# Splitting each expert pair's weights where they are used, and starting the routed stage one shared chunk earlier

## The reference

```python
x = x + 0.5 * ffn(layernorm(x)); x = x + attn(layernorm(x)); x = x + 0.5 * ffn(layernorm(x))

# ffn(flat), flat [4096, 128]
probs = softmax(flat @ gate_W.T)
top_v, top_i = top_k(probs, 2)
out_e  = (silu(flat @ w1_e[e]) * (flat @ w3_e[e])) @ w2_e[e]
routed = sum(gates[:, e] * out_e[e])
shared = sum((silu(flat @ w1_s[n]) * (flat @ w3_s[n])) @ w2_s[n]) / 8
return 0.5 * shared + 0.5 * routed

# attn(x)
q, k, v = split(rms_norm(x) @ w_qkv.T); q = rms_norm(q); k = rms_norm(k)
y = sigmoid(q) * cumsum(exp(k) * v) / (cumsum(exp(k)) + 1e-6)
u, g = split(y @ w_swiglu.T); return x + (u * silu(g)) @ w_out.T
```

## Time and profile before

| | us |
|---|---|
| median of 3 runs | 748.2 (746.82 to 748.32) |
| the profiled execution, its time | 750.38 |
| the profiled execution, its span | 748.7 |
| PE busy | 664.1 (89% of the span) |
| DVE busy | 463.5 (62%) |
| POOL busy | 445.3 (59%) |
| ACT busy | 411.0 (55%) |
| mean granted clock of PE | 0.963 of full speed |

### The profile page before, as it was taken

The page is one execution under the profiler, slowest core; times in us unless marked ns, Lnnn a source line. Parts: engine busy times, 40 slices in busy tenths (PEclk is TensorE's granted clock), DMA queues, the critical chain, the costliest instruction groups (busy, mean ns, idle before and its releaser), DMA issues.

```text
span 748.7 us, 14295 instructions
## 1 busy us (share of the span) xinstructions
PE 664.1 (89%) x4860; PEld 604.9 (81%) x4860; DVE 463.5 (62%) x1169; ACT 411.0 (55%) x861; POOL 445.3 (59%) x519
## 2 busy tenths in 40 slices
PE   3878929999999999966887777999999999999996
PEld 3667829999999999944664565788999999999973
DVE  6678884555444555447999885975455545454435
ACT  2658504666666666326664526663666666666520
POOL 5600396677777777459997515006577777777530
PEclk9989959999999999989999997999999999999998
DMA  9551001112222132031100000602121221112146
GB/s 299 217 88 27 2 15 44 43 50 55 53 53 54 51 55 54 30 123 42 42 30 1 0 1 1 116 2 44 36 55 55 51 54 51 54 53 52 39 130 228
DMA packets 35686, 45.91 MB, mean 61 GB/s; under 512 B 6433, under 2 KB 27937, under 8 KB 35233
## 3 DMA queue, kind: packets, MB, share of 16 engines
q1 hardware_dynamic: 25632, 24.39, 11.5%
q0 software_dynamic: 9984, 20.63, 11.3%
HBM read 28.41 MB, written 16.58 MB: 60 GB/s over the span
## 4 chain that ended last, share of the span: by engine, by line
PE 66%; DVE 20%; ACT 3%; issue 3%; POOL 3%; DMA 2%; SPq 1%; POOLq 0%; DVEq 0%; ACTq 0%
PE psY L1487 18%; PE psU L1336 6%; PE psU L1335 6%; PE psU L1334 6%; PE psG L1334 6%; PE psG L1336 6%; PE psG L1335 6%; PE psH L1405 5%; DVE rec L1076 3%; PE psT L1433 2%; DVE XN L747 2%; DVE hs L757 2%; DVE ln_stats L734 1%; DVE xn L1060 1%; POOL results L650 1%
## 5 line engine op out<-in xcount | busy, mean ns | idle before, releaser
L1155 ACT ACTIVATE silu<-psG 128x512 f32<-128x512 f32 x220 | 131.1, 596 | 168.3 <-PE psG L1336 147.9
L635 POOL DMA_INDIRECT rows<-tokens,source x156 | 150.3, 964 | 104.4 <-issue 45.3
L954 DVE TENSOR_TENSOR hT<-silu,psU 128x512 f32<-128x512 f32 x156 | 107.4, 688 | 157.9 <-PE psU L1336 151.5
L650 POOL DMA_INDIRECT results<-yout,target x156 | 153.4, 983 | 64.0 <-issue 45.7
L1487 PE MATMUL psY<-W,hT 128*128 x1232 | 162.3, 275 | 1.8 <-DVE yout L980 1.8
L1487 PEld LDWEIGHTS psY<-W,hT 128*128 128x128 f32 x1232 | 150.4, 191 | 2.1 <-DVE hT L954 2.1
L1229 ACT ACTIVATE w_high<-W13H 128x1024 fp32r x78 | 82.7, 1060 | 55.5 <-PE psU L1336 55.4
L1334 PE MATMUL psG<-xTH,w_high 128*128 128x256 f32 x312 | 100.0, 321 | 0.0
L1336 PE MATMUL psG<-xTH,w_low 128*128 128x256 f32 x312 | 88.0, 282 | 0.0
L1336 PE MATMUL psU<-xTH,w_low 128*128 128x256 f32 x312 | 88.0, 282 | 0.0
L1335 PE MATMUL psU<-xTL,w_high 128*128 128x256 f32 x312 | 87.7, 281 | 0.0
(11 more groups left out here) (188 smaller groups left out, 1245.3 us busy)
## 6 DMA issues: line engine op xcount, KB each, us to landing
W<-w_e SPq DMA_DIRECT2D x3, 2048.0 KB, 13.8
tokens<-XN SPq DMA_DIRECT2D x16, 260.0 KB, 6.0
Y<-results SPq DMA_DIRECT2D x32, 128.0 KB, 2.2
YF<-results SPq DMA_DIRECT2D x16, 256.0 KB, 5.7
rows<-tokens,source POOLq DMA_INDIRECT x156
results<-yout,target POOLq DMA_INDIRECT x156, 2.3
X<-x SPq DMA_DIRECT2D x8, 256.0 KB, 5.5
out<-X SPq DMA_DIRECT2D x8, 256.0 KB, 2.8
```

The lines of the kernel that those rows point to most:

```text
L635: pool.indirect_dma_start(rows[:, slot(l, g), t, :], None, tokens, bass.IndirectOffsetOnAxis(ap=source[:, tile:tile + 1], axis=0))\
L650: pool.indirect_dma_start(results, bass.IndirectOffsetOnAxis(ap=target[:, tile:tile + 1], axis=0), yout[:, g % 2, t, :], None).then_inc(y_ ...
L954: dve.tensor_tensor(hT[:, s.u // PT % 2, half, :].rearrange("p f c -> p (f c)"), silu[:, s.u % 2, :], psU[:, s.u % 2, :], ALU.mult).then_i ...
L1155: act.activation(silu[:, s.u % 2, :], psG[:, s.u % 2, :], ACT.Silu).then_inc(silu_done, 1)
```

## The change

`FRONT` becomes `[6, 5]`: one chunk of shared steps moves from ahead of the routed stage to behind it, in each layer. The copies `W13H` and `W13L` and the instructions that make them go. `W13` stays in fp32, with a memory of its own, and each pair's weights are split on the way to their homes: ACT rounds 128x1024 of `W13` into `w_high`, and DVE subtracts that from `W13` into `w_low`. For this DVE, too, loads each pair's offset into a register. The rounding of the transposed rows (`xTH`) goes from DVE to ACT. The first two pairs are split before the routed stage begins: on ACT after shared step 22 in layer 0 and 18 in layer 1, on DVE after the front's last step. `w_high`, `w_low` and the buffer `Y` share the memory of `YF`. POOL no longer has anything between the low parts of the tokens and its fetches.

```diff
-WCOLS = 1024
-WPARTS = E * F // WCOLS
-FRONT = [7, 6]
+FRONT = [6, 5]
...
-        W13H = sb("W13H", [P, 2, E * F], fp32r)
-        memory = overlaid([("W13", [P, 2, E * F], fp32)], [("YF", [P, TOPK, TILES, D], fp32)],
-                          [("W13L", [P, 2, E * F], fp32r)])
+        W13 = sb("W13", [P, 2, E * F])
+        memory = overlaid([(f"w_{part}{n}", [P, 2, F], fp32r) for n in range(2) for part in ("high", "low")] +
+                          [("Y", [P, 4, TOPK, TB, D], fp32)], [("YF", [P, TOPK, TILES, D], fp32)])
...
-                if l == 0:
-                    pool.wait_ge(place_made, BATCHES_P)
-                    for j in range(2 * WPARTS):
-                        w, cols = j % 2, bass.ds(j // 2 * WCOLS, WCOLS)
-                        pool.wait_ge(high_made, j + 1)
-                        pool.tensor_tensor(W13L[:, w, cols], W13[:, w, cols],
-                                           W13H[:, w, cols].bitcast(fp32), ALU.subtract).then_inc(w_split, 1)
...
-                    dve.tensor_copy(xTH[:, par, :, :].rearrange(flat), psT[:, :]).then_inc(xT_link, 1)
-                    dve.wait_ge(xT_link, g + (GROUPS * l + 1))
+                    dve.wait_ge(xT_high, g + (GROUPS * l + 1))
...
+                def low_weights(p):
+                    if p >= PAIRS:
+                        return
+                    dve.wait_ge(pair_high, PAIRS * l + p + 1)
+                    dve.tensor_tensor(w_low[p % 2][:, :, :], W13[:, :, bass.ds(entries[p], F)],
+                                      w_high[p % 2][:, :, :].bitcast(fp32), ALU.subtract).then_inc(pair_split, 1)
...
+                    if k == front[l]:
+                        dve.wait_ge(w_off_done, l + 1)
+                        for p in range(PT):
+                            look_up(p)
+                            low_weights(p)
...
-                pipelined(dve, [(gated_routed, 4), (copy_y, 6), (copy_xT_later, 0)], RUN, 2 * GT,
+                pipelined(dve, [(look_up_later, 4), (gated_routed, 4), (copy_y, 6), (low_later, 4), (copy_xT_later, 0)], RUN, 2 * GT,
...
+                def high_xT(g):
+                    act.wait_ge(xT_psum, GROUPS * l + g + 1)
+                    act.activation(xTH[:, g % 2, :, :].rearrange("p t c -> p (t c)"), psT[:, :], ACT.Copy)\
+                       .then_inc(xT_high, 1)
+                def high_weights(p):
+                    if p >= PAIRS:
+                        return
+                    if p >= PT:
+                        act.wait_ge(u_full, first_routed[l] + PT * (p - 1))
+                    act.activation(w_high[p % 2][:, :, :], W13[:, :, bass.ds(entries[p], F)], ACT.Copy)\
+                       .then_inc(pair_high, 1)
...
-                    if l == 0 and part < 2 * WPARTS:
-                        cols = bass.ds(part // 2 * WCOLS, WCOLS)
-                        act.activation(W13H[:, part % 2, cols], W13[:, part % 2, cols], ACT.Copy).then_inc(high_made, 1)
+                    if k == front[l] + 1:
+                        high_xT(0)
+                    if k == min(TABLE_STEP[l] + 3, front[l] - 1):
+                        act.wait_ge(w_off_done, l + 1)
+                        act.wait_ge(experts_in, 48)
+                        for p in range(PT):
+                            look_up(p)
+                            high_weights(p)
...
                 for k in range(RUN):
+                    if k % PT == PT - 1:
+                        look_up(k // PT + PT)
                     silu_of(Step.of(k, 2), first_routed[l] + k)
-                    if k % PT == 1:
-                        weights_of(k // PT + PT, 0)
-                    elif k > 0:
-                        weights_of(k // PT - 1 + PT, 1)
+                    if k % GT == 0 and k // GT + 1 < GROUPS:
+                        high_xT(k // GT + 1)
+                    if k % PT == PT - 1:
+                        high_weights(k // PT + PT)
...
-                        pe.wait_ge(pair_weights, PT * (PAIRS * l + s.i // PT + 1))
+                        pe.wait_ge(pair_split, PAIRS * l + s.i // PT + 1)
```

More of the change, by code:

```diff
@@ L192, in macaron @@
         X = sb("X", [P, TILES, D])
-        W13H = sb("W13H", [P, 2, E * F], fp32r)
-        memory = overlaid([("W13", [P, 2, E * F], fp32)], [("YF", [P, TOPK, TILES, D], fp32)],
-                          [("W13L", [P, 2, E * F], fp32r)])
-        W13, W13L, YF = memory["W13"], memory["W13L"], memory["YF"]
+        W13 = sb("W13", [P, 2, E * F])
+        memory = overlaid([(f"w_{part}{n}", [P, 2, F], fp32r) for n in range(2) for part in ("high", "low")] +
+                          [("Y", [P, 4, TOPK, TB, D], fp32)], [("YF", [P, TOPK, TILES, D], fp32)])
+        w_high = [memory[f"w_high{n}"] for n in range(2)]
+        w_low = [memory[f"w_low{n}"] for n in range(2)]
+        YF, Y = memory["YF"], memory["Y"]
         W2 = sb("W2", [P, E * FT * D])
@@ L318, in macaron @@
              ("ha", [P, 2, TB * P], fp32)],
-            [("rows", [P, RING, GT, ROW], fp32),
-             ("gap", [P, 4 * CH * P - RING * GT * ROW], fp32),
-             ("w_low1", [P, 2, F], fp32r),
-             ("last_chunks", [P, (CHUNKS - 6) * CH * P], fp32),
-             ("w_high0", [P, 2, F], fp32r),
-             ("w_low0", [P, 2, F], fp32r),
-             ("w_high1", [P, 2, F], fp32r)],
+            [("rows", [P, RING, GT, ROW], fp32)],
             [("XNTL", [P, NT], fp32r), ("XNTH", [P, NT], fp32r)])
@@ L342, in macaron @@
         rows = memory["rows"]
-        w_high = [memory[f"w_high{n}"] for n in range(2)]
-        w_low = [memory[f"w_low{n}"] for n in range(2)]
         psG = ps("psG", [P, 2, 512])
@@ L955, in gated_routed, with look_up_later, low_later @@
                                       psU[:, s.u % 2, :], ALU.mult).then_inc(h_done, 1)
+                def look_up_later(s):
+                    if s.i % PT == PT - 1:
+                        look_up(s.i // PT + PT)
+                def low_later(s):
+                    if s.i % PT == PT - 1:
+                        low_weights(s.i // PT + PT)
                 def copy_xT_later(s):
@@ L1029, in _ @@
                     gated_shared(Step.of(k, 2 * FT))
+                    if k % FT == 6 % FT and k // FT > FRONT[0]:
+                        add_shared(k // FT - 1)
                 add_shared(CHUNKS - 1)
@@ L1216, in _ @@
                         batches += 1
-                def weights_of(p, part):
-                    if p >= PAIRS:
-                        return
-                    if part == 0 and p < PT:
-                        act.wait_ge(u_full, shared_at(l, (4 + 2 * p) * FT - 1) + 1)
-                    elif part == 0:
-                        act.wait_ge(u_full, first_routed[l] + PT * (p - 1))
-                    if p not in entries:
-                        entries[p] = act.value_load(w_off[0:1, p:p + 1], min_val=0, max_val=(E - 1) * F)
-                    kept, used = ((W13H, w_high), (W13L, w_low))[part]
-                    act.activation(used[p % 2][:, :, :], kept[:, :, bass.ds(entries[p], F)], ACT.Copy)\
-                       .then_inc(pair_weights, 1)
-                entries = {}
-                act.wait_ge(w_off_done, l + 1)
-                act.wait_ge(w_split, 2 * WPARTS)
-                for p in range(PT):
-                    weights_of(p, 0)
-                    weights_of(p, 1)
                 for k in range(RUN):
+                    if k % PT == PT - 1:
+                        look_up(k // PT + PT)
                     silu_of(Step.of(k, 2), first_routed[l] + k)
-                    if k % PT == 1:
-                        weights_of(k // PT + PT, 0)
-                    elif k > 0:
-                        weights_of(k // PT - 1 + PT, 1)
+                    if k % GT == 0 and k // GT + 1 < GROUPS:
+                        high_xT(k // GT + 1)
+                    if k % PT == PT - 1:
+                        high_weights(k // PT + PT)
                 for k in range(front[l], SHARED):
```

24 lines of the change are left out of this document (14 added, 10 removed).

## The result

| | before | after |
|---|---|---|
| median of 11 runs each, side by side | 748.25 us (746.82 to 749.54) | 750.3 us (748.12 to 750.9) |
| ratio | 1 | 1.0024, 95% interval 1.0012 to 1.0035 |
| profiled execution: time, span | 750.38, 748.7 | 750.3, 748.6 |
| mean granted clock | 0.963 | 0.979 |

The changed kernel is 0.24% slower, by about 2 us; 735.2 was predicted. The profiled execution of before lay 2 us above its median and that of after on its median, so a comparison of the two traces adds up to 0 and not to 2 us.

The account below looks back on a forecast made before the run. PE, busy 89% of the span, was taken as the bound, so gains come from its waits or clock. Terms −17.1 + 3.6 + 3.4 + 0.8 − 3.7 = −13.0 us took the median 748.2 to 735.2 us, range 730 to 744.

Parts of the forecast that it names:

- table of layer 0, its slow clock, ACT's batches: Layer 0's front: PE's 13.1 us wait, 2.8 of slow clock and 1.2 behind ACT's copies go; −17.1 us.
- wait for rows at the front's end: Before each routed stage: PE waits about 2.2 us for fetched rows; net +1.8 a layer, +3.6 us.
- slow clock after these waits: After the waits for rows: PE's clock at its lower level for 4 us, 1.7 a layer; +3.4 us, or 0.
- split in the routed stage: Routed stage: ACT's rounding and DVE's 1.2 us subtraction per pair leave PE's path unchanged; 0 us.
- POOL's pace: Routed stage: POOL takes 10.27 us a group against PE's 9.67 and has less lead; +0.4 a layer, +0.8 us.
- behind layer 0's routed stage: After layer 0's routed stage: the moved chunk's cover buys nothing, as attention already begins after the last shared chunk.
- tail of layer 1: End of layer 1: a third chunk covers the YF wait; 2.01 us wait and 1.7 slow clock go, −3.7 us.
- rival B: Routed stages: DVE's two-SBUF-input subtractions hold up POOL's DMAs; 34 us in all, 769 us; chance 0.12.
- 28d: Routed stage: each subtraction holds a POOL DMA for d, 2d a group over 14 groups; d taken as 0.6 us.
- a lead that is lived on: Routed stage: POOL falls back 0.6 us a group and lives on its start, in layer 1 13.5 us, then 6.5.
- 0.6 us to spare: Tightest place, the scaling at 284.13: results landed at 283.5; PE would bear some 0.5 us more.
- the first two pairs are covered: Front's end: splitting the first pairs takes 3.1 us beside PE's out_shared of 3.84; nothing, up to +1 a layer.

Follow-up runs that it names:

- e7: Kernel before, with the eight W13L subtractions made by DVE behind steps 20 to 27 of layer 0 instead of by POOL; 735.08 us.
- e1: Kernel after, but from the third pair on ACT also copies weights to psH in PSUM, and DVE subtracts w_high from that; 733.91 us, ratio 0.9814.
- e2: Kernel after, with w_low a plain DVE copy of W13 (one SBUF operand) instead of the subtraction; 747.02 us, ratio 0.9991.
- e6: Kernel of e1 (low parts from PSUM) with FRONT [7, 5] instead of [6, 5]; 732.57 us, ratio 0.9793.
- e4: Kernel after, with each DVE subtraction of 128x1024 made as two of 128x512; 749.41 us, ratio 1.0028.
- e3: Kernel after, with FRONT back at [7, 6] and each pair still split on its way by ACT and DVE; 746.59 us, ratio 0.9983.
- e8: Kernel of e3 with a ring of four groups of rows instead of three, results six groups behind; 747.82 us, ratio 0.9989.
- e9: Kernel of e8 with SEND_LAG = RING + 1, so results are again five groups behind the fetches; 746.2 us, ratio 0.9977.
- e11: Kernel after, with yout in three parts instead of two, a scaling waiting for the results of three groups before; 744.28 us, ratio 0.9948.
- e5: Kernel before, with w_low filled by DVE instead of ACT, by an operation of 128x1024 reading two SBUF operands; 776.29 us, ratio 1.0373.
- e10: Kernel of e6 with the rounding xTH given back to DVE, as in the kernel before; 732.46 us, ratio 0.9801.

## Why the prediction was wrong

By its own terms, measured in the two traces:

| term | predicted | measured |
|---|---|---|
| table of layer 0, its slow clock, ACT's batches | −17.1 | −17.1 |
| wait for rows at the front's end, net of 0.41, both layers | +3.6 | +3.3 |
| slow clock after these waits | +3.4 | 0 |
| split in the routed stage, and POOL's pace | 0 and +0.8 | +18.5 |
| behind layer 0's routed stage | 0 | −0.9 |
| tail of layer 1 | −3.7 | −3.9 |
| sum | −13.0 | −0.1 |

(−17.1 is 121.30 − 97.27 = 24.03, less the chunk of 9.08, plus the wait of 2.14. 18.5 is the 8.93 and 8.71 of the two routed stages plus the 0.41 a layer that had stood in them and belongs to the second row. The first row is not luck: it had been said as 13.1 + 2.8 + 1.2, and e7, which takes away the first two alone, measured 15.8. The −0.9 was not followed up; in that stretch the clock stood at its lower level from 328 to 335 us before, and from 324.5 to 328 after.)

**The step that failed** is the split in the routed stage, for which the sum takes 0. It looked at the path from ACT over DVE to PE, which indeed has room (PE never waits for `w_low`), and left POOL out of the sum. The price stood in rival B, and B's arithmetic holds: it had 28d a layer over the groups up to the tightest. With the measured mean d of 0.28 us (20.0 us over 72 holds) that is 7.8 us a layer, and the routed stages grew by 8.9 and 8.7. B said that it decides from d = 0.23. Its d of 0.6 was too large: since a held DMA ends 0.85 us behind the subtraction and takes 0.975 by itself, even random meetings would cost about 0.5 us each (an estimate from these rows), and they are not random, because the holds themselves set their phase. That 735.2 + 56 x 0.28 = 750.9 lies so near the measured 750.3 is partly luck: the slow clocks of +3.4 in it did not come, and the stages grew by more than 28d. So the forecast and B differed in one number that no row of before showed, and I gave B 12% because `gate_parts` had not lengthened a fetch. That was weak evidence, as the text itself said: an operation of 0.17 us is too short to show a hold, since even in one of 1.22 us a DMA that began 1.04 us into it took under 0.1 us more.

One reading that pointed the right way was at hand: DVE's table slowed to the length of POOL's subtractions, which shows that the two engines exclude each other. The fetch of 1.19 us beside the table says less than B made of it: the first fetch of layer 0 takes 1.17 us in the kernel after too (at 90.70), beside DVE's short operations at the end of the table. The Trainium skill (SBUF — State Buffer, Who interferes with whom) has both sentences that the prediction weighed. The one by which a DVE instruction with two SBUF inputs contends with GpSimd's reads holds here: 72 DMAs held by up to a microsecond. The one by which `tensor_tensor` did not stall DMAs does not, and the measurement decides. By the same section a DVE instruction with at most one input in SBUF, outside its fast modes, does not contend, and one in them does: e1 and e2 agree, with no hold and with holds of up to 0.4 us, if the copy of 128x1024 in 0.69 us is such a mode (the subtraction of 128x512 takes as long, 0.69 us in e4).

**POOL's pace** was right where nothing was held and the front was short: e1 shows one group of 10.1 us in each layer and e6 one in layer 1, the predicted 0.4. Its picture of a lead that is lived on was incomplete. The lead counts only up to the first send; after it POOL has the room of `yout`'s two halves (e3, e8, e9, e11). Hence the small step between "0.6 us to spare" and 9 us lost a layer: the room is used up once, and then each group shows in full.

**The slow clock** after the waits for rows was counted with 1.7 us each and did not come in the kernel after. Where it did come, in layer 1 of e11, it cost 1.6 us, so the size was right and its coming was not. The windows over both waits and what follows (us, PE busy, PEld, DVE, ACT, POOL, granted clock, DMA share, GB/s):

```profile
94.00:98.00 4.00, 1.86 (x12) 1.31 (x12) 2.30 (x4) 2.52 (x4) 3.09 (x4) 1.00 0.24 52
98.00:102.00 4.00, 4.00 (x38) 4.00 (x37) 3.19 (x6) 0.56 (x1) 3.08 (x4) 1.00 0.23 50
...
504.00:508.00 4.00, 2.04 (x14) 1.49 (x13) 2.79 (x4) 2.49 (x4) 3.04 (x4) 1.00 0.23 50
508.00:512.00 4.00, 4.00 (x38) 4.00 (x37) 2.95 (x6) 0.42 (x1) 2.84 (x3) 1.00 0.23 50
```

**All other steps held**: the first two pairs are covered, no wait of PE for `w_low`, `w_low` 1.22 us for an estimated 1.2, the wait for `YF` gone and the stretch from 710 to 740 at clock 1.00. Without the slow clock the sum is −16.4, which makes 731.8 us; e1, which has everything but the holds and groups 0.07 us longer (+2.5 us over 36 of them), took 733.9.

## What to carry to other kernels

Before work goes to DVE beside a POOL that issues indirect DMAs, look where its operands lie. An operation that reads SBUF alone can hold a DMA that starts inside it past its own end; the same operation with one operand in PSUM was free here, and a copy on ACT to get it there was cheap. And two engines that hold each other fall into step, so that the loss is not the mean of chance meetings: price it with both ends, and look for the buffer that gives the slower one its room (here `yout`), since a lead beyond it is worth nothing.

## What was not expected of the hardware

A hold ends at a fixed distance: in four kernels (after, e2, e3, e5) a held DMA's record ends 0.80 to 0.88 us after DVE's instruction, whatever its length (0.69 or 1.22 us) and wherever in it the DMA began, but for the first and last 0.05 us. In e5 those that began in the last tenth of a microsecond, which are hardly held at all, end up to 0.93 us after it.

PE's clock after a short wait is not told by the wait's length. In the kernel after, waits of 2.14 and 1.96 us left it at 1.00. In e11 a wait of 1.87 us at the same place in layer 1 was followed by slower work, `out_shared` in 5.04 us instead of 3.74, and in e10 one of 2.82 by this:

```profile
497.99 1.11 PE L1456 MATMUL psT<-ident,rows 128*128 128x128 f32 x4 [2.82 <-DMA rows<-tokens,source]
498.89 6.17 PE L1428 MATMUL psH<-W2S,hs 128*128 128x128 f32 x32
```

```profile
498.00:502.00 4.00, 4.00 (x19) 4.00 (x20) 3.02 (x6) 0.00 (x0) 2.85 (x4) 0.50 0.23 50
```

The clock was at 0.50 there, the lower level, and `out_shared` took 2.4 us more. What decides between the two was not tried.
